# A gated delta attention layer and its feed-forward part on one core: v turned by VectorE, one x buffer, new orders on every engine, phases overlapped

## Chip, core and metric

One core of a Trainium2 chip. The metric is the device time of one execution in microseconds (us). The engines are PE (TensorE), DVE (VectorE), ACT (ScalarE), POOL (GpSimd) and SP (SyncE, which issues all transfers here). Each runs its own list of instructions in order and waits on semaphores that others raise.

## What is computed

The reference, cut to its core (16 sequences of 256 tokens, 256 channels, 32 heads with 64 by 64 state, all float32):

```
qkvz = layernorm(x) @ w_qkvz.T          # per head q, k, v, z
q, k, v = causal depthwise conv of 4 taps along the tokens
g = -exp(A_log) * softplus(a + dt_bias);  beta = sigmoid(b)
q, k = l2norm(q) / 8, l2norm(k)
for each token:                          # state S: 64 x 64 per head
    S = S * exp(g);  delta = (v - k S) * beta
    S = S + k delta;  o = q S
o = o * rsqrt(mean(o*o) + eps) * norm_weight * sigmoid(z)
x = x + layernorm(o @ w_out.T)
x = x + layernorm(down(silu(gate(layernorm(x))) * up(layernorm(x))))
```

## The kernel before, in words

The work is cut in three phases, each a block of code of its own with a barrier behind it. Phase 1 normalizes x, transposes it to `xT_d` in DRAM and computes the gates of all heads. Phase 2 is the attention. It loops over 8 groups of 4 heads and, within a group, over 8 blocks of 512 tokens (2 sequences): 64 steps. Phase 3 is the feed-forward part, 8 blocks of 512 tokens.

A step of phase 2 has 16 units (`G`) of 64 tokens and two heads side by side on the partitions, in chunks c = 0 to 3 of each sequence. Its work, by the names in the code:
- PE `project(s)`, s = 0 to 7: k, q, v and z, two slots each; four matmuls of 512 columns each into a PSUM bank (banks 0 to 3 are shared out by hand). ACT takes the first tap of the convolution out of the bank (`first_tap`); for k and v DVE adds the other three (`conv`, L958), for q ACT writes products (`tap_product`) and POOL adds them (`add_tap`, L703).
- PE `k_tokens`, `v_tokens` (L1174): k and v turned so that tokens lie on the partitions, as 32 small matmuls with a unit matrix for each half. DVE scales them out of PSUM (`scale_k`, `scale_v`).
- PE `scores` (L1193), from which DVE takes `a_mat` and `p_t` (`matrices`). The matrix 1 + A of each unit has to be inverted. Its 16 by 16 blocks go through DRAM to a layout with one block per partition (`units_out`, `units_in`), where DVE does forward substitution, 15 columns of two small operations each (`substitute`, L972 and L976, parts 0 to 5, marked by `sub_done0` to `sub_done5`). ACT turns the result (`turn_units`), it goes back through DRAM (`z_out`, `z_back`), and PE joins the blocks (`join16_inner`, `join16_outer`, `join_inner`, `join_outer`).
- The recurrence over chunks, a chain that runs from engine to engine: PE `solve(c)` (L1250), ACT `delta_out`, PE `advance` (L1260), DVE `new_state` (L1026, L1028) and `decay_state`, PE `key_state` for c + 1 (L1240), DVE `residual` (L1013, L1016), PE `solve(c + 1)`; beside it PE `output` (L1273, L1275).
- PE `sum_squares`, `project_out` (L1288); DVE adds to `acc`, which holds the output of all heads for all tokens in SBUF.
- POOL `differences` (L691), `mask` (L695) and `scale_decays` on the decay matrices, `scale_q`, `clamp`, `end_decays`.

The order of all this is written out by hand. Each engine has a `turn(s)`, where s[0] to s[3] are the four steps in flight, s[0] the newest, and the engine takes from each the pieces in the order in which they stand. `wait_for(engine, semaphore, step, n)` waits for that step's count. So an operation that waits holds back all that stands behind it in the turn of its engine. In the turn before, for one step:

```
wait_for(dve, st_full[1], s[3], 1)
new_state(s[3], 1)
...
substitute(s[2], 5, range(12, 15))
...
residual(s[3], 2)
decay_state(s[3], 2)
...
conv(s[1], 0, banks[2])
```

The x block of a step is loaded to one of two tiles `xT`, and the gates (`gcrow`, `gcb`) to single tiles by `load_gates`.

## Time and profile before

| | |
|---|---|
| median of 3 runs | 3398.41 us (3397.84 to 3399.98) |
| the profiled execution | 3400.17 us, span 3398.1 us |
| mean granted clock of TensorE | 0.985 of full speed |
| PE busy | 3208.9 us, 94% |
| DVE busy | 2460.7 us, 72% |
| ACT busy | 1747.8 us, 51% |
| POOL busy | 1094.2 us, 32% |
| DMA queues | 27.3% of 16 engines' span |

The span is the time from the first to the last instruction that the profiler recorded; the time of an execution is a little longer. Busy shares are means over the three phases. Phase 1 lasts to about 85 us, phase 2 to 3008 us, phase 3 to the end. In a row of the timeline the first number is the start in us from the start of the span, the second the time taken, "xN" the number of instructions merged, and what stands in brackets is how long the engine was idle before it and what released it.

### The profile page before, as it was taken

The numbers are of one execution on the slowest core, as the hardware profiler recorded it, in microseconds if no ns is written. First come the engines' busy times: TensorE is split into PE (matmuls) and PEld (weight loads), VectorE is DVE, ScalarE is ACT, GpSimd is POOL, SyncE is SP. The second block draws the span as 40 slices with busy tenths as digits, with TensorE's granted clock in tenths as the row PEclk, the third lists the DMA queues.
The fourth block names the chain that finished last, engine by engine and source line by source line (L and its number), as shares of the span: only waits on it lengthen the run. The fifth ranks groups of instructions, "written<-read, shape, count | busy, mean of one in ns | idle before, by whom it ended". The sixth has DMA issues, their size and how long they took to land. (4 is left out here: it accounts for less than half of the span.)

```text
span 3398.1 us, 116966 instructions
## 1 busy us (share of the span) xinstructions
PE 3208.9 (94%) x51008; PEld 2185.0 (64%) x51008; DVE 2460.7 (72%) x5802; ACT 1747.8 (51%) x3306; POOL 1094.2 (32%) x904
## 2 busy tenths in 40 slices
PE   6799999999999999999999999999999999879998
PEld 3466666666666666666666666666666666645554
DVE  6577777777777777777777777777777777645555
ACT  5455555555555555555555555555555555423333
POOL 1433333333333333333333333333333333100000
PEclk8899999999999999999999999999999999979999
DMA  5323232232233233322333223222233222110000
GB/s 143 57 50 61 51 52 44 49 66 52 52 52 65 46 51 52 59 49 50 52 68 53 50 46 66 52 44 49 50 68 52 52 52 45 28 56 25 19 19 19
DMA packets 757483, 175.67 MB, mean 52 GB/s; under 512 B 707568, under 2 KB 728432, under 8 KB 755824
## 3 DMA queue, kind: packets, MB, share of 16 engines
q1 hardware_dynamic: 756976, 168.19, 26.4%
q8 instruction: 406, 6.65, 0.8%
q14 instruction: 101, 0.83, 0.1%
HBM read 120.13 MB, written 39.58 MB: 47 GB/s over the span
## 5 line engine op out<-in xcount | busy, mean ns | idle before, releaser
L1164 PE MATMUL bank<-xT,w_sb 128*128 128x512 f32 x2048 | 1020.7, 622 | 13.2 <-DMA xT<-xT_d 8.3
L703 POOL TENSOR_TENSOR kq<-kq,products 128x510 f32<-128x510 f32 (+2 forms) x384 | 445.2, 1166 | 885.7 <-ACT kq L779 600.5
L1164 PEld LDWEIGHTS bank<-xT,w_sb 128*128 128x128 f32 x2048 | 349.7, 190 | 299.7 <-issue 252.9
L958 DVE SCALAR_TENSOR_TENSOR kq<-bank,cw,kq 128x510 f32<-128x510 f32 (+2 forms) x384 | 286.8, 747 | 166.5 <-ACT kq L779 149.1
L691 POOL TENSOR_TENSOR dec_a<-gcrow,gcb 128x1024 f32<-128x1024 f32 x64 | 121.7, 1902 | 835.7 <-DMA gcb<-gcb_d 835.7
L958 DVE SCALAR_TENSOR_TENSOR v_c<-bank,cw,v_c 128x510 f32<-128x510 f32 (+2 forms) x384 | 285.2, 743 | 9.1
L976 DVE TENSOR_TENSOR x_un<-x_un,prod_un 128x15 f32<-128x15 f32 (+7 forms) x960 | 258.3, 269 | 32.9
L972 DVE TENSOR_TENSOR prod_un<-a_un,x_un 128x15 f32<-128x15 f32 (+7 forms) x960 | 255.8, 266 | 31.2 <-DMA a_un<-a_d 4.3
L1193 PE MATMUL bank<-kq 64*64 64x128 f32 x4096 | 271.3, 272 | 5.3 <-issue 2.8
L1288 PE MATMUL bank<-wo,u_sq 128*128 128x256 f32 x1024 | 260.3, 398 | 2.8 <-DVE u_sq L1035 2.8
L785 ACT ACTIVATE products<-bank,cw 128x512 f32<-128x512 f32 x384 | 246.0, 701 | 0.0
L1275 PEld LDWEIGHTS bank<-p_t,delta 64*64 64x64 f32 x4096 | 215.2, 136 | 47.8 <-issue 47.8
L1275 PE MATMUL bank<-p_t,delta 64*64 64x64 f32 x4096 | 243.3, 220 | 0.0
L1273 PEld LDWEIGHTS bank<-q_g,state 64*64 64x64 f32 x3072 | 179.6, 134 | 95.4 <-issue 95.4
L1193 PEld LDWEIGHTS bank<-kq 64*64 64x64 f32 x4096 | 230.7, 134 | 8.5 <-issue 8.5
L838 ACT COPY delta<-bank 128x256 f32<-128x256 f32 x256 | 94.4, 369 | 247.2 <-PE bank L1250 247.2
L1288 PEld LDWEIGHTS bank<-wo,u_sq 128*128 128x128 f32 x1024 | 187.8, 193 | 34.2 <-DVE u_sq L1035 4.4
L1273 PE MATMUL bank<-q_g,state 64*64 64x64 f32 x3072 | 205.8, 226 | 1.1 <-ACT delta L838 1.1
L779 ACT ACTIVATE kq<-bank,cw 128x512 f32<-128x512 f32 x256 | 169.7, 688 | 67.1 <-PE bank L1164 67.1
L1250 PE MATMUL bank<-rhs,z_t 64*64 64x64 f32 x3072 | 128.0, 222 | 72.5 <-DVE rhs L1016 72.5
L1250 PEld LDWEIGHTS bank<-rhs,z_t 64*64 64x64 f32 x3072 | 106.9, 134 | 126.9 <-issue 126.9
L1005 DVE TENSOR_TENSOR a_mat<-bank,dec_a 128x256 f32<-128x256 f32 x256 | 106.4, 416 | 110.1 <-PE bank L1193 110.0
(159 smaller groups left out, 6007.3 us busy)
## 6 DMA issues: line engine op xcount, KB each, us to landing
xT<-xT_d SPq DMA_DIRECT2D x64, 512.0 KB, 3.8
gcrow<-gcrow_d SPq DMA_DIRECT2D x128, 256.0 KB, 4.6
a_d<-a_mat SPq DMA_DIRECT2D x256, 64.0 KB, 2.1
z_t<-z_d SPq DMA_DIRECT2D x256, 64.0 KB, 2.5
w_sb<-in_w_qkvz SPq DMA_DIRECT2D x8, 1024.0 KB, 6.1
x_un<-eye_un SPq DMA_DIRECT2D x64, 128.0 KB, 3.8
a_un<-a_d SPq DMA_DIRECT2D x64, 128.0 KB, 4.7
z_d<-t_un SPq DMA_DIRECT2D x64, 128.0 KB, 3.0
```

What stands on the lines that cost most here:

```text
L703: nc.gpsimd.tensor_tensor(t[:, :, d:SEQ], t[:, :, d:SEQ], prod[:, :, 0:SEQ - d], ALU.add).then_inc(tap_added[i], 1)
L779: ins = nc.scalar.activation(dst, bank[:, :], ACT.Identity, scale=cw_two[m.grp % 2][:, s * TAPS + TAPS - 1:s * TAPS + TAPS])
L785: ins = nc.scalar.activation(products[i % 4][:, :], bank[:, :], ACT.Identity, scale=cw_two[m.grp % 2][:, w:w + 1])
L958: ins = nc.vector.scalar_tensor_tensor(t[:, :, d:SEQ], src[:, :, 0:SEQ - d], cw_two[m.grp % 2][:, w:w + 1], t[:, :, d:SEQ], ALU.mult, ALU.add)
L972: own.need(own.mark(nc.vector.tensor_tensor(prod, a_un[:, j + 1:B, j:j + 1].broadcast_to([P, rows, wid]), x_un[:, j:j + 1, 0:wid].broadcas ...
L976: ins = nc.vector.tensor_tensor(rest, rest, prod, ALU.subtract)
L1164: ins = nc.tensor.matmul(bank[:, :], w_two[m.grp % 2][:, h, s * P:(s + 1) * P], xT[m.par][:, h, :], start=(h == 0), stop=(h == HT - 1))
L1193: ins = nc.tensor.matmul(bank[half, i * P:(i + 1) * P], kq[half, k, s // 2, t0:t0 + C], kq[half, k:q + 1:q - k, s // 2, t0:t0 + C], start= ...
L1250: ins = nc.tensor.matmul(banks[4][half, 256 + i * C:256 + (i + 1) * C], z_t[m.par][half, g, :], rhs[half, i, :] if c else v_r[m.par][half, ...
L1273: nc.tensor.matmul(o, state[c % 2][half, i, :], q_g[m.par][half, g, :], start=True, stop=False)
L1275: ins = nc.tensor.matmul(o, delta[half, i, :], p_t[m.par][half, g, :], start=(c == 0), stop=True)
L1288: ins = nc.tensor.matmul(bank[:, t * HID:(t + 1) * HID], u_sq[:, a, (2 * k + t) * P:(2 * k + t + 1) * P], wo[m.grp % 2][:, a, :], start=(a ...
```

## The change

v is no longer turned by PE. DVE transposes it in blocks of 32 by 32 (`turn_v`) from `v_c` to a new tile `v_x`, and eight transfers per step (`v_turned`) move the blocks from `v_x` to their places in `v_r`, within SBUF; `scale_v` then scales `v_r` in place. There is one tile `xT` instead of two, loaded after projection 5 of the step before. Banks 0 to 3 are given out in turn (`ring`), 18 uses per step instead of 20. The turn of every engine is written in a new order. `solve(0)`, `advance(0)` and `key_state(1)` stand a turn later, with s[3]. The first x block for phase 2 is loaded in phase 1, and the first normalizations and transposes of phase 3, with its weights, are done within the last steps of phase 2 (phase 3 uses other tiles for that).

```
-        xT = [sb(f"xT{i}", [P, HT, TB]) for i in range(2)]
+        xT = sb("xT", [P, HT, TB])
...
-        products = [sb(f"products{i}", [P, TB]) for i in range(4)]
+        product = sb("product", [P, 4, TB])
+        products = [product[:, i, :] for i in range(4)]
...
+        v_x = sb("v_x", [P, G, C])
...
+                    sp.wait_ge(xT_out[0], 8 * NSP)
+                    sp.dma_start(xT[:, :, :].rearrange("p h t -> p (h t)"), xT_d[0]).then_inc(x_T_in, 16)
...
+        def ring(m, place):
+
+            return banks[(18 * m.off + place) % 4]
...
+        wgu = [[flat(xT), flat(product)[:, 0:INTER]], [flat(w_two[1])[:, 0:INTER], flat(w_two[1])[:, INTER:2 * INTER]]]
+        wdn = flat(w_sb).rearrange("p (i h) -> p i h", h=HID)
+        xt = gcrow[:, :, :].rearrange("p g c -> p (g c)").rearrange("p (t h) -> p t h", h=HID)
+        xn = dec_a[:, :, :].rearrange("p g c -> p (g c)").rearrange("p (t h) -> p t h", h=HID)
...
+                        if m.off:
+                            sp.dma_start(xT[:, :, :].rearrange("p h t -> p (h t)"), xT_d[m.index() % NSP]).then_inc(x_T_in, 16)
...
+                        if m.off == STEPS - 1:
+                            sp.dma_start(first_x, x.rearrange("(s t p) h -> s p t h", p=P, t=TT)[0]).then_inc(xr_in, 16)
...
+                    def v_turned(m):
+                        for h in range(2):
+                            for f in range(2):
+                                for t in range(2):
+                                    r, q = D * h + W2 * t, D * h + W2 * f
+                                    sp.dma_start(v_r[m.par][r:r + W2, :, W2 * f:W2 * f + W2], v_x[q:q + W2, :, W2 * t:W2 * t + W2]) \
+                                        .then_inc(v_f_in, 16)
...
-                        if s[3]:
-                            identity_in(s[3])
-                            wait_for(sp, mats_done[0], s[3], 1)
+                        if s[2]:
+                            wait_for(sp, proj_full[5], s[2], 1, back=1)
+                            load_x(s[2])
+                        if s[3]:
+                            wait_for(sp, mats_done[3], s[3], 1)
                             units_out(s[3])
                         if s[2]:
-                            wait_for(sp, qg_done[1], s[2], 1, back=1)
+                            wait_for(sp, eend_done, s[2], 1, back=1)
                             load_gates(s[2])
                         if s[3]:
                             wait_for(sp, a_d_out, s[3], 64)
                             units_in(s[3])
+                            wait_for(sp, vx_done[1], s[3], 1)
+                            v_turned(s[3])
                             wait_for(sp, zt_done, s[3], 1)
                             z_out(s[3])
-                            x_out(s[3])
                             wait_for(sp, z_d_out, s[3], 16)
                             z_back(s[3])
+                            x_out(s[3])
+                        if s[2]:
+                            wait_for(sp, x_d_out, s[2], 16, back=1)
+                            identity_in(s[2])
+                        if s[3]:
                             wait_for(sp, x_d_out, s[3], 16)
                             x_back(s[3])
-                        if s[1]:
-                            load_x(s[1])
 
                     pipeline(sp, turn)
+
+                    for i in proj_full:
+                        sp.wait_ge(proj_full[i], STEPS)
+                    for i in (2, 5):
+                        sp.wait_ge(tap_added[i], STEPS)
+                    for h in range(HT):
+                        for u in range(2):
+                            sp.dma_start(wgu[h][u], w_gu[:, h, u * INTER:(u + 1) * INTER]).then_inc(wf_in, 16)
+                    sp.dma_start(wdn, w_dn).then_inc(wf_in, 16)
 
...
+                    def turn_v(m, a):
+                        ins = nc.vector.transpose(v_x[:, a * GP:(a + 1) * GP, :].rearrange("p g c -> p (g c)"), v_c[:, a, :])
...
 
-                    def scale_v(m, a, bank):
+                    def scale_v(m, a):
                         g = slice(a * GP, (a + 1) * GP)
-                        ins = nc.vector.tensor_tensor(v_r[m.par][:, g, :], bank[:, :].rearrange("p (g c) -> p g c", c=C), col(br[:, g]).broadcast_to([P, GP, C]), ALU.mult)
-                        if a in vr_done:
...
 
+                    def first_transposes():
+                        pe.wait_ge(xn_ready, 1)
+                        for h in range(HT):
+                            for t in range(TT):
+                                ins = nc.tensor.transpose(banks[(5, 4)[h]][:, t * P:(t + 1) * P], first_n[:, t, h * P:(h + 1) * P], ident[:, :])
+                            ins.then_inc(xT_ready, 1)
+
                     def sum_squares(m, a, bank):
+                        if m.off == STEPS - 1 and a == 1:
+                            first_transposes()
                         nc.tensor.matmul(bank[:, :], ones[:, 0, :], u_sq[:, a, :], start=True, stop=True).then_inc(ss_full[a], 1)
 
```

The turns of DVE, POOL and PE, at three places. Names: `x_un` and `prod_un` are the substitution, `rhs` the residual, `s_dec` the decayed state, `kq` the tile of k and q, `st_full`, `ks_full`, `rhs_done` and so on the semaphores.

DVE before, the end of the substitution and what follows:

```order
L972 TENSOR_TENSOR prod_un<-a_un,x_un 128x15
L976 TENSOR_TENSOR x_un<-x_un,prod_un 128x15
L1013 TENSOR_TENSOR rhs<-bank,b_eg 128x256
L1016 TENSOR_TENSOR rhs<-v_r,rhs 128x256
L1019 TENSOR_TENSOR s_dec<-state,e_end 128x256
L958 SCALAR_TENSOR_TENSOR kq<-bank,cw,kq 128x2x255
L958 SCALAR_TENSOR_TENSOR kq<-bank,cw,kq 128x2x254
L958 SCALAR_TENSOR_TENSOR kq<-bank,cw,kq 128x2x253
L1026 TENSOR_TENSOR state<-bank,s_dec 128x256
```

DVE now, from the residual of chunk 1 to new_state 1:

```order
L1121 TENSOR_TENSOR rhs<-v_r,rhs 128x256
L1071 TENSOR_TENSOR prod_un<-a_un,x_un 128x39
L1075 TENSOR_TENSOR x_un<-x_un,prod_un 128x3x13
L1071 TENSOR_TENSOR prod_un<-a_un,x_un 128x28
L1075 TENSOR_TENSOR x_un<-x_un,prod_un 128x2x14
L1071 TENSOR_TENSOR prod_un<-a_un,x_un 128x15
L1075 TENSOR_TENSOR x_un<-x_un,prod_un 128x15
L1056 SCALAR_TENSOR_TENSOR kq<-bank,cw,kq 128x2x255
L1056 SCALAR_TENSOR_TENSOR kq<-bank,cw,kq 128x2x254
L1056 SCALAR_TENSOR_TENSOR kq<-bank,cw,kq 128x2x253
L1129 TENSOR_TENSOR state<-bank,s_dec 128x256
```

Part 5 of the substitution stood ahead of residual 2, whose new_state 1 was done before; now it stands behind residual 1, and conv 1 and new_state 1 stand behind it.

POOL before, from the differences of a step to its mask and the next add:

```order
L691 TENSOR_TENSOR dec_a<-gcrow,gcb 128x1024 [waits gc_in,deca_done]
L703 TENSOR_TENSOR kq<-kq,products 128x2x255 [waits tap_done2]
L703 TENSOR_TENSOR kq<-kq,products 128x2x254 [waits tap_added0]
L703 TENSOR_TENSOR kq<-kq,products 128x2x255 [waits tap_prod3]
L695 TENSOR_TENSOR dec_p<-dec_a,masks 128x1024
L703 TENSOR_TENSOR kq<-kq,products 128x2x254 [waits tap_prod4,tap_added3]
```

POOL now:

```order
L748 TENSOR_TENSOR dec_a<-gcrow,gcb 128x1024 [waits gc_in]
L760 TENSOR_TENSOR kq<-kq,product 128x2x255 [waits tap_done2]
L760 TENSOR_TENSOR kq<-kq,product 128x2x254 [waits tap_prod1,tap_added0]
L760 TENSOR_TENSOR kq<-kq,product 128x2x253 [waits tap_added1]
L752 TENSOR_TENSOR dec_p<-dec_a,masks 128x1024
L760 TENSOR_TENSOR kq<-kq,product 128x2x255 [waits tap_prod3]
```

The three adds of the first half of q now stand together, and the mask behind them, with nothing of the other half between.

PE before, around the turning of v:

```order
L1222 MATMUL bank<-z_t,a_mat 32x32 x31
L1174 MATMUL bank<-masks,v_c 64x64 [waits mats_done1]
L1174 MATMUL bank<-masks,v_c 64x64 x15
L1174 MATMUL bank<-masks,v_c 64x64 [waits mats_done0]
L1174 MATMUL bank<-masks,v_c 64x64 x15
L1231 MATMUL bank<-p,x_top 32x32 [waits p1_done,xtop_done]
```

PE now, from solve 1 to the k tokens; the groups on `v_c` are gone, and key_state 2 waits for `state_done1`, which DVE raises behind conv 1:

```order
L1360 MATMUL bank<-rhs,z_t 64x64 x7
L1278 MATMUL bank<-xT,w_sb 128x512 [waits z_exp0]
L1278 MATMUL bank<-xT,w_sb 128x512
L1370 MATMUL bank<-delta,kt 64x64 [waits delta_done1]
L1370 MATMUL bank<-delta,kt 64x64 x7
L1287 MATMUL bank<-masks,kq 64x64 [waits tap_prod1]
L1287 MATMUL bank<-masks,kq 64x64 x15
L1350 MATMUL bank<-state,kq 64x64 [waits state_done1]
L1350 MATMUL bank<-state,kq 64x64 x7
L1287 MATMUL bank<-masks,kq 64x64 [waits conv_done1]
```

## Rows read from the trace of the kernel before

**Rows 1.** One step: us; busy PE, PEld, DVE, ACT, POOL; clock; DMA share; GB/s.

```profile
1603.25:1647.64 44.39, 43.36 (x774) 30.22 (x773) 34.16 (x81) 24.45 (x46) 16.95 (x14) 1.00 0.29 50
```

**Rows 2.** Timeline of PE in the same step.

```profile
1635.90 2.08 PE L1174 MATMUL bank<-masks,v_c 64*64 64x64 f32 x64
1637.91 1.20 PE L1231 MATMUL bank<-p,x_top 32*32 32x32 f32 x64
1639.04 1.98 PE L1164 MATMUL bank<-xT,w_sb 128*128 128x512 f32 x4
1640.95 0.68 PE L1250 MATMUL bank<-v_r,z_t 64*64 64x64 f32 x16
1641.56 1.99 PE L1288 MATMUL bank<-wo,u_sq 128*128 128x256 f32 x8
```

**Rows 3.** Waits of PE, 184 to 2920 us: us in total, times, longest.

```profile
PE bank L1250 <- DVE rhs L1016: 63.7, 62, 1.0
```

**Rows 4.** Groups of DVE instructions: busy, mean ns, idle before.

```profile
L958 DVE SCALAR_TENSOR_TENSOR kq<-bank,cw,kq 128x510 f32<-128x510 f32 (+2 forms) x384 | 286.8, 747 | 166.5 <-ACT kq L779 149.1
...
L1045 DVE STREAM_TRANSPOSE x_top<-z_t 128x512 f32<-128x512 f32 x64 | 44.6, 697 | 2.1 <-ACT z_t L822 2.1
```

**Rows 5.** DMA issues: count, KB each, median us to landing.

```profile
z_t<-z_d SPq DMA_DIRECT2D x256, 64.0 KB, 2.5
...
gcb<-gcb_d SPq DMA_DIRECT2D x64, 16.0 KB, 5.0
```

**Rows 6.** Timeline of ACT in a steady step.

```profile
1605.36 0.37 ACT L838 COPY delta<-bank 128x256 f32<-128x256 f32 x1 [3.77 <-PE bank L1250]
1605.63 1.06 ACT L763 ACTIVATE dec_a<-dec_p 128x1024 f32<-128x1024 f32 x1
1606.58 0.59 ACT L773 ACTIVATE z_tmp<-bank 128x512 f32<-128x512 f32 x1
...
1607.27 0.63 ACT L804 ACTIVATE l_z<-z_tmp 128x512 f32<-128x512 f32 x1
1607.79 1.84 ACT L785 ACTIVATE products<-bank,cw 128x512 f32<-128x512 f32 x3
1609.50 0.71 ACT L779 ACTIVATE kq<-bank,cw 128x512 f32<-128x512 f32 x1
```

**Rows 7.** Timeline of POOL at three places.

```profile
129.48 1.90 POOL L691 TENSOR_TENSOR dec_a<-gcrow,gcb 128x1024 f32<-128x1024 f32 x1 [11.40 <-DMA gcb<-gcb_d]
...
1610.29 2.50 POOL L703 TENSOR_TENSOR kq<-kq,products 128x510 f32<-128x510 f32 x2 [9.79 <-ACT kq L779]
...
1618.39 2.36 POOL L695 TENSOR_TENSOR dec_p<-dec_a,masks 128x1024 f32<-128x1024 f32 x1
```

**Rows 8.** Timeline of DVE at the same times.

```profile
129.88 1.53 DVE L972 TENSOR_TENSOR prod_un<-a_un,x_un 128x15 f32<-128x15 f32 x1 [4.25 <-DMA a_un<-a_d]
...
1607.88 0.43 DVE L1026 TENSOR_TENSOR state<-bank,s_dec 128x256 f32<-128x256 f32 x1 [1.64 <-PE bank L1260]
...
1610.28 0.22 DVE L972 TENSOR_TENSOR prod_un<-a_un,x_un 128x55 f32<-128x55 f32 x1
1610.54 1.16 DVE L976 TENSOR_TENSOR x_un<-x_un,prod_un 128x55 f32<-128x55 f32 x1
1611.73 1.12 DVE L972 TENSOR_TENSOR prod_un<-a_un,x_un 128x48 f32<-128x48 f32 x1
```

**Rows 9.** Timeline of PE where phase 2 fills.

```profile
169.11 0.68 PE L1240 MATMUL bank<-state,kq 64*64 64x64 f32 x16 [1.69 <-DVE state L1028]
169.72 3.62 PE L1164 MATMUL bank<-xT,w_sb 128*128 128x512 f32 x4
```

**Rows 10.** Timeline of SP and PE at the change to phase 3.

```profile
3008.33 0.39 SPq L1452 DMA_DIRECT2D gcrow<-in_x  x1
...
3020.22 1.97 PE L1634 MATMUL bank<-ident,dec_a 128*128 128x128 f32 x8 [12.87 <-DMA w_sb<-in_w_dn]
3022.86 1.22 PE L1644 MATMUL bank<-q_sq,v_r 128*128 128x512 f32 x1 [0.67 <-ACT q_sq L1494]
```

More of the change, by code:

```diff
@@ L853, in turn @@
                         if s[1]:
-                            wait_for(act, proj_full[1], s[1], 1)
-                            first_tap(s[1], 1, banks[1])
+                            wait_for(act, diff_done, s[1], 1)
+                            magnitudes(s[1])
+                        if s[2]:
+                            wait_for(act, z_clamped[1], s[2], 1)
+                            log_z(s[2], 1)
                         if s[3]:
@@ L948, in _, with moments, normed, first_norms @@
                     own = Own(dve, dve_self)
+                    first = [acc[:, t, :] for t in range(TT)]
+                    def moments():
+                        ks = [own.mark(nc.vector.bn_stats(stats[:, t, :], first[t])) for t in range(TT)]
+                        for t in range(TT):
+                            own.need(ks[t])
+                            k = own.mark(nc.vector.bn_aggr(mv[:, t, :], stats[:, t, :]))
+                        own.need(k)
+                        nc.vector.tensor_scalar(rstd, mv[:, :, 1], EPS_LN, None, ALU.add).then_inc(var_ready, 1)
+                    def normed(dst, n):
+                        dve.wait_ge(rstd_ready, n + 1)
+                        for t in range(TT):
+                            ins = nc.vector.tensor_scalar(dst[:, t, :], first[t], mv[:, t, 0:1], rstd[:, t:t + 1],
+                                                          ALU.subtract, ALU.mult)
+                        return ins
+                    def first_norms():
+                        k = own.mark(normed(at, 0))
+                        dve.wait_ge(xr_in, 16)
+                        own.need(k)
+                        nc.vector.tensor_tensor(acc[:, 0:TT, :], first_x, at, ALU.add).then_inc(x1_done, 1)
+                        dve.wait_ge(x1_done, 1)
+                        dve.sem_inc(dve_gate, 1)
+                        moments()
                     def tail(m):
@@ L1149, in turn @@
                             substitute(s[1], 0, range(0, 2))
+                            wait_for(dve, sub_done[0], s[1], 1)
+                            substitute(s[1], 1, range(2, 4))
+                            wait_for(dve, sub_done[1], s[1], 1)
+                            substitute(s[1], 2, range(4, 6))
+                            wait_for(dve, sub_done[2], s[1], 1)
+                            substitute(s[1], 3, range(6, 9))
+                        if s[2]:
+                            wait_for(dve, st_full[0], s[2], 1)
+                            new_state(s[2], 0)
                         own.turn()
@@ L1294, in turn @@
                         if s[1]:
-                            wait_for(pe, vr_done[0], s[1], 1, back=1)
-                            project(s[1], 6, banks[0])
+                            wait_for(pe, conv_done[0], s[1], 1)
+                            wait_for(pe, tap_done[0], s[1], 1)
+                            project(s[1], 6, ring(s[1], 2))
+                        if s[3]:
+                            wait_for(pe, zoff_done, s[3], 1)
+                            solve(s[3], 0)
+                        if s[1]:
+                            wait_for(pe, conv_done[4], s[1], 1)
+                            wait_for(pe, tap_done[4], s[1], 1)
+                            project(s[1], 2, ring(s[1], 3))
+                        if s[3]:
+                            wait_for(pe, delta_done[0], s[3], 1)
+                            advance(s[3], 0)
+                        if s[1]:
+                            project(s[1], 1, ring(s[1], 0))
                         if s[3]:
                             output(s[3], 0)
+                            wait_for(pe, state_done[0], s[3], 1)
+                            key_state(s[3], 1)
+                        if s[1]:
+                            project(s[1], 3, ring(s[1], 1))
+                        if s[3]:
                             wait_for(pe, rhs_done[1], s[3], 1)
@@ L1456, in store @@
                         sp.dma_start(out.rearrange("(s t p) h -> s p t h", p=P, t=TT)[i], yo).then_inc(y_out, 16)
-                    load(0)
-                    for h in range(HT):
-                        for u in range(2):
-                            sp.dma_start(wgu[h][u], w_gu[:, h, u * INTER:(u + 1) * INTER]).then_inc(wf_in, 16)
-                    sp.dma_start(wdn, w_dn).then_inc(wf_in, 16)
                     load(1)
```

441 lines of the change are left out of this document (205 added, 236 removed).

## The prediction

> **What bounds the kernel now.** I first read busy time over one steady step [rows 1]: PE works 43.36 of 44.39 us, DVE 34.16, ACT 24.45, POOL 16.95. PE bounds, and what it still waits for is one thing: in the list of waits 62 steps each lose 1.03 us before a solve, to DVE's residual (`rhs`, L1016), 63.7 us in all [rows 3]. There are 64 steps; 62 x 44.39 = 2752 us of the span of 3398.1 are such steps. So I price one step, times 62, then the two phase changes. The profiled execution took 3400.17 us, 2.1 above its span and 1.8 above the median of 3398.41; I add 0.3 to a span to get a median.
>
> **The change, part by part, in one step.**
>
> PE loses `v_tokens`: 64 matmuls; from their first start to the next group's is 2.01 us [rows 2]: **-2.01**. Everything else on PE is only reordered. If no wait remained, the old one goes too: **-1.03**, and a step would be 41.35 us.
>
> DVE gets two block transposes of v, 0.70 us each by the same operation on `x_top` [rows 4]; the scaling of v stays, with its input now in SBUF. 34.2 + 1.4 = 35.6 us of work in 41.35: it fits, by the sum. It is hidden if no order puts it in front of PE.
>
> SP gets eight 64 KB transfers per step, in pieces of 128 B, the shape of `z_t<-z_d`, which lands in 2.5 us [rows 5]. Issued at about 0.5 us each behind `units_in`, they land some 7 us after the last of v is turned, and v is not read before the middle of the next step: nothing, with more than 10 us of cover. The single `xT` is loaded after projection 5, 10 us ahead of projection 0: nothing.
>
> **The order around `sub_done5`** is what I think decides. I walk one step of the new order from t = 0, the start of projection 6. On PE a projection takes 1.91 from start to start, and a group of 16 small matmuls 0.61 [rows 2]; output 0 is such a group, and 32 token matmuls are half of v's 64, 1.00. The row before `key_state(2)` is then: projection 6 at 0, solve 0 at 1.91, projection 2 at 2.52, advance 0 at 4.43, projection 1 at 5.04, output 0 at 6.95, key_state 1 at 7.56, projection 3 at 8.17, solve 1 at 10.08, projection 7 at 10.69, advance 1 at 12.60, k tokens 0 at 13.21, **key_state 2 at 14.21**.
>
> ACT: delta 0 goes out when solve 0 has ended, at 2.64; then, with the spacings of [rows 6] (0.27 for delta, 0.95 for 1024 columns, 0.52 for 512, 0.2 for the two small ones, 0.57 for a tap), decays, square_q and log_z end at 5.3, and two products, the exponential, tap 1 and tap 2 follow: tap 2 of q is done at 8.45.
>
> POOL then runs without a gap, since all it needs is there: three adds of q's taps, 1.2 each as a pair takes 2.50, then the mask, 2.36 [rows 7]: **busy from 8.5 to 14.5**.
>
> DVE: accumulate ends at 0.7, nine columns of substitution (18 operations 0.25 apart [rows 8]) last until 5.3, new_state 0 takes 0.43 [rows 8], substitution 4 (6 operations) ends at 7.2, decay 1 at 7.6. The residual waits for key_state 1 (ends 8.24), so its second half is issued at 8.7, and substitution 5 (6 operations) after it. Both of those read two tiles of SBUF. The rows show what such an operation costs while POOL works: 0.22 us becomes 1.16 and 1.12, one behind each of two adds, and 1.53 behind a POOL operation of 1.90 that it ends with, to 0.03 [rows 7, 8]. So DVE gets one operation through per POOL operation. The residual ends at 10.1 behind the first add; substitution 5 gets its first three through behind add 2 (11.1), add 3 (12.3) and the mask (14.6), the last three free, 15.4. Without POOL it would end at 10.6. Behind it stand conv 1 (3 x 0.747 = 2.24 [rows 4]) and new_state 1 (0.43), so PE can start key_state 2 at 18.2 with 0.15 for the handover, not at 14.2: **+4.0**, bounds 3.6 and 4.4 (0.2 on either side for where the first operation slips in, and as much for the walk). The old order had its two collisions here too, and lost 1.9 us on DVE, 1.03 on PE; it had the mask elsewhere.
>
> The Trainium skill (SBUF — State Buffer, Who interferes with whom) says that a VectorE operation with two SBUF inputs and a GpSimd one that reads SBUF exclude each other for a whole instruction; for the mask, which no row here shows against DVE, it is the only direct word. By it the wait is 4.0 us; if two engines merely shared, the step would be 41.35.
>
> ACT's `turn_units` waits for `sub_done5` too, and taps of k behind it come 5 us later; PE, held by the same 4.0, meets them without a new wait. After that, `add_squares` stands next to POOL's scaling of q and the sum of squares waits for it: **+0.3**, between 0 and 0.6 (half an add of POOL).
>
> **The clock.** After 1.69 us of waiting and shortly before that another short one, TensorE's projection group takes 3.62 us where it takes 1.98 [rows 2, 9]; two levels, 1.2 and 2.4 GHz. A step with a wait of 4.0 us would pay something like it each time: 1.64 for a projection; less where small matmuls follow, which also load weights. I take **+1.3**, bounds 0 and 1.7. In the steady stretch now the clock is at full speed [rows 1] with 1.03 us waits. The Trainium skill (TensorE: Matmul & The Clock Gate, The HAM clock gate) ties the fall to a stretch of idleness; read strictly, a wait this long need not contain one, and the sum would be without the 1.3. The row shows a fall after less, so I keep it.
>
> **Phase changes.** Phase 3 starts at 3008.33, its first gate matmul runs at 3022.86 after 12.87 us for `w_dn` and the transposes [rows 10]. Weights and first block are now ready: -14.5. Given back: solve 0, advance 0 and key_state 1 of the last step lose the cover of the output projections (about 2), and the first transposes (1.97 [rows 10], partly under a wait) stand before the last sum of squares: +3.5 in all. The earlier first x load I count at nothing, as gates and decays still come after the barrier. **-11**, bounds -15 and -5.
>
> **Sum.** -2.01 - 1.03 + 4.0 + 0.3 + 1.3 = +2.56 per step; x 62 = +159; -11; +0.3: 3398.1 + 148 = **3546 us**. Its own range by the bounds: 3420 (3.6, 0, 0 and -15) to 3625.
>
> **Rivals.**
> 1. *The stall, but the clock holds.* +1.26 per step: +78 - 11, 3466 us. For it: the wait may be too short or split; against: [rows 9]. 0.16.
> 2. *Other side: DVE gets past POOL.* If ACT is late enough, POOL's burst starts after 10.6, or substitution 5 is through before the mask. The point of decision is tap 2 of q: 8.45 in my walk, 10.6 needed. Then a loss like today's 1.03 remains: -2.01 per step, -125 - 11, 3263 us; with none, 3198. For it: the walk carries errors of some tenths in each of 20 places, POOL's `differences` waits for a gate transfer (5 us from issue, [rows 5]) and holds up ACT when late. Against: `magnitudes` has almost 2 us of slack before it moves tap 2. 0.28.
> 3. *Half of it.* Only the mask or only the adds hit, a wait of 1.9: -1.14 per step, 3316 us. 0.06.
> 4. *The change does not do what it says*: v or `a_un` arrives late behind the eight transfers, and DVE's waits take back just what PE saves, 3.04 per step less the phases' share: 3398 us; for it only the growth in small pieces, against it the cover above. 0.04.
>
> My forecast itself has 0.46. Faster: 2 and 3, 0.34. Within 0.2% (about what a measurement of this kernel can tell from no change): 4, 0.04. Slower: 0.62. The likeliest case gives 3546 with 3420 to 3625 as its own range; for 8 in 10 the range has to take in rival 2's 3263 but not its tail down to 3198 (0.12), and ends at 3600 (0.05 above): 3255 to 3600.
>
> **What would show it.** Right: in the list of waits PE `key_state` waiting for DVE's state some 4 us in each of 62 steps; substitution operations of over 1 us, four to a step where there are two now, one over 2; a step of 46 to 47.5 us; granted clock under 1.00 in steady windows; no PE time on v's transposes; PE's gap at the phase change under 3 us. Wrong if POOL's adds start after substitution 5 has ended, or a small DVE operation inside the mask takes 0.2 us. If the step is near 41.5, the lock was not where I put it; if it is 45.6 with clock 1.00, only the clock term was wrong.

## The result, and the profile after

| | before | after |
|---|---|---|
| median | 3398.12 us (4 runs, 3395.34 to 3399.98) | 3480.27 us (4 runs, 3466.01 to 3485.81) |
| ratio | | 1.0235, 95% interval 1.0212 to 1.0257: slower |
| profiled execution | 3400.17, span 3398.1 us | 3481.44, span 3479.7 us |
| mean granted clock | 0.985 | 0.956 |

The prediction was 3546 (3255 to 3600), slower with 0.62. To see where 81.6 us of span came from, I take the same group of PE in each step, the outer join (`join_outer`), and measure from the start of one to the start of the next. After the change there are 59 steps between the third and the 62nd group, at 244.98 and 2983.18 us: 46.41 us each. Before, between the second and the 63rd at 207.02 and 2932.01 us, 61 steps: 44.67. So a step costs 1.74 us more, 62 x 1.74 = 108, and everything else gives back 26.

The page after, its busy times and its clock in 40 slices:

```profile
PE 3123.6 (90%) x46912; PEld 2137.2 (61%) x46912; DVE 2797.8 (80%) x5930; ACT 1752.6 (50%) x3306; POOL 1128.0 (32%) x904
...
PEclk9999999999999999999999999999999999989999
```

PE has 85 us less work than before and waits more; DVE went from 2460.7 to 2797.8. Two stretches of one step each (columns as in [rows 1]):

```profile
1603.07:1648.82 45.75, 42.05 (x709) 29.46 (x708) 39.41 (x83) 25.12 (x48) 17.47 (x14) 0.96 0.36 60
1648.82:1694.57 45.75, 41.93 (x726) 29.03 (x726) 40.62 (x87) 25.47 (x48) 17.48 (x14) 1.00 0.36 60
```

The clock was 1.00 in [rows 1]; now it is below that in 50 of the 59 steps and whole in nine. PE's longest waits, 400 to 2900 us (total, times, longest), where [rows 3] had 1.0 at a time:

```profile
PE bank L1350 <- DVE state L1129: 191.0, 54, 3.9
...
PE bank L1360 <- DVE rhs L1121: 8.1, 45, 0.2
```

It is `key_state(2)`, once in every step, 191.0 / 54 = 3.54 us. The timelines of PE, POOL and DVE at this place, in the first of the two stretches:

```profile
1611.11 0.68 PE L1370 MATMUL bank<-delta,kt 64*64 64x64 f32 x16
1611.63 1.10 PE L1287 MATMUL bank<-masks,kq 64*64 64x64 f32 x32
1616.43 1.12 PE L1350 MATMUL bank<-state,kq 64*64 64x64 f32 x16 [3.70 <-DVE state L1129]
1617.31 1.94 PE L1287 MATMUL bank<-masks,kq 64*64 64x64 f32 x32
```

```profile
1607.76 3.63 POOL L760 TENSOR_TENSOR kq<-kq,product 128x510 f32<-128x510 f32 x3 [11.22 <-ACT kq L845]
1611.35 2.35 POOL L752 TENSOR_TENSOR dec_p<-dec_a,masks 128x1024 f32<-128x1024 f32 x1
```

```profile
1607.25 0.42 DVE L1121 TENSOR_TENSOR rhs<-v_r,rhs 128x256 f32<-128x256 f32 x1
1607.59 0.19 DVE L1071 TENSOR_TENSOR prod_un<-a_un,x_un 128x39 f32<-128x39 f32 x1
1607.82 1.26 DVE L1075 TENSOR_TENSOR x_un<-x_un,prod_un 128x39 f32<-128x39 f32 x1
1609.11 1.11 DVE L1071 TENSOR_TENSOR prod_un<-a_un,x_un 128x28 f32<-128x28 f32 x1
1610.26 0.19 DVE L1075 TENSOR_TENSOR x_un<-x_un,prod_un 128x28 f32<-128x28 f32 x1
1610.48 0.94 DVE L1071 TENSOR_TENSOR prod_un<-a_un,x_un 128x15 f32<-128x15 f32 x1
1611.45 2.28 DVE L1075 TENSOR_TENSOR x_un<-x_un,prod_un 128x15 f32<-128x15 f32 x1
1613.65 2.30 DVE L1056 SCALAR_TENSOR_TENSOR kq<-bank,cw,kq 128x510 f32<-128x510 f32 x3
1615.87 0.41 DVE L1129 TENSOR_TENSOR state<-bank,s_dec 128x256 f32<-128x256 f32 x1
```

Read it from the bottom: PE waits for state 1 (L1129), which stands behind the second convolution of k (L1056), which stands behind substitution part 5. Four of its six operations take 1.26, 1.11, 0.94 and 2.28 us instead of about 0.2. They end at 1609.08, 1610.22, 1611.42 and 1613.73: after one, two and all three of POOL's adds (3.63 / 3 = 1.21 each, the last ends at 1611.39) and with the mask (1613.70). The convolution reads a bank and SBUF; here it runs almost wholly after POOL's burst, and experiment 1 shows it beside POOL's adds with the same 2.30 us. Behind the wait PE's groups of 16 and 32 small matmuls take 1.12 and 1.94 instead of 0.68 and 1.10: the low level of the clock.

### The profile page after: what moved, and what is told of

The parts are those of the page before. It is cut to its first block and busy times, and to the rows that moved or that the text cites. A ratio compares the mean times of both kernels' runs of the same rounds, so it can differ in the third digit from the quotient of the medians.

```text
span 3479.7 us, 109296 instructions
## 1 busy us (share of the span) xinstructions
PE 3123.6 (90%) x46912; PEld 2137.2 (61%) x46912; DVE 2797.8 (80%) x5930; ACT 1752.6 (50%) x3306; POOL 1128.0 (32%) x904
## 5 line engine op out<-in xcount | busy, mean ns | idle before, releaser
L1278 PE MATMUL bank<-xT,w_sb 128*128 128x512 f32 x2048 | 995.0, 614 | 12.6 <-PEq L507 5.2
L760 POOL TENSOR_TENSOR kq<-kq,product 128x510 f32<-128x510 f32 (+2 forms) x384 | 443.7, 1156 | 747.1 <-ACT kq L845 556.2
L1071 DVE TENSOR_TENSOR prod_un<-a_un,x_un 128x15 f32<-128x15 f32 (+7 forms) x960 | 370.5, 386 | 27.9 <-DMA a_un<-a_d 1.5
L1350 PE MATMUL bank<-state,kq 64*64 64x64 f32 x3072 | 144.2, 238 | 221.2 <-DVE state L1129 217.8
L1056 DVE SCALAR_TENSOR_TENSOR v_c<-bank,cw,v_c 128x510 f32<-128x510 f32 (+2 forms) x384 | 286.3, 746 | 33.5 <-ACT v_c L845 24.5
L1056 DVE SCALAR_TENSOR_TENSOR kq<-bank,cw,kq 128x510 f32<-128x510 f32 (+2 forms) x384 | 286.3, 746 | 26.7 <-ACT kq L845 17.5
L1303 PE MATMUL bank<-kq 64*64 64x128 f32 x4096 | 277.1, 277 | 20.3 <-issue 17.1
L1385 PEld LDWEIGHTS bank<-p_t,delta 64*64 64x64 f32 x4096 | 241.2, 148 | 47.0 <-issue 47.0
L1350 PEld LDWEIGHTS bank<-state,kq 64*64 64x64 f32 x3072 | 124.5, 151 | 228.5 <-issue 228.5
L774 POOL TENSOR_TENSOR dec_a<-dec_a,cols 128x1024 f32<-128x1024 f32 x64 | 121.7, 1902 | 436.5 <-DVE b_eg L1102 436.4
L851 ACT ACTIVATE product<-bank,cw 128x512 f32<-128x512 f32 x384 | 250.7, 691 | 1.5 <-PE bank L1278 1.5
L771 POOL TENSOR_TENSOR q_g<-kq,gcrow 128x512 f32<-128x512 f32 x128 | 177.3, 1385 | 118.6 <-ACT gcrow L836 113.5
L1383 PEld LDWEIGHTS bank<-q_g,state 64*64 64x64 f32 x3072 | 210.7, 150 | 1.4 <-issue 1.3
```

What stands on the lines that cost most here:

```text
L760: nc.gpsimd.tensor_tensor(t[:, :, d:SEQ], t[:, :, d:SEQ], prod[:, :, 0:SEQ - d], ALU.add).then_inc(tap_added[i], 1)
L771: nc.gpsimd.tensor_tensor(q_g[m.par][:, a * GP:(a + 1) * GP, :], half_of(m, 1)[:, a, :].rearrange("p (g c) -> p g c", c=C), gcrow[:, a * G ...
L851: ins = nc.scalar.activation(products[i % 4], bank[:, :], ACT.Identity, scale=cw_two[m.grp % 2][:, w:w + 1])
L1056: ins = nc.vector.scalar_tensor_tensor(t[:, :, d:SEQ], src[:, :, 0:SEQ - d], cw_two[m.grp % 2][:, w:w + 1], t[:, :, d:SEQ], ALU.mult, ALU.add)
L1071: own.need(own.mark(nc.vector.tensor_tensor(prod, a_un[:, j + 1:B, j:j + 1].broadcast_to([P, rows, wid]), x_un[:, j:j + 1, 0:wid].broadcas ...
L1278: ins = nc.tensor.matmul(bank[:, :], w_two[m.grp % 2][:, h, s * P:(s + 1) * P], xT[:, h, :], start=(h == 0), stop=(h == HT - 1))
```

## The experiments

Twelve runs of eleven kernels, each timed beside the kernel before on the same chip, which took 3396.0 us beside experiments 1 to 4, 3399.7 beside 5 to 8 and 3399.6 beside 9 to 12. The changed kernel was not timed again beside them, so totals are compared with its 3480.27 across chips. "Step" is the mean distance between outer joins from the third to the 62nd.

**1. Substitution part 5 earlier.** In DVE's turn:

```
                             substitute(s[2], 4, range(9, 12))
+                            wait_for(dve, sub_done[4], s[2], 1)
+                            substitute(s[2], 5, range(12, 15))
                         if s[3]:
                             decay_state(s[3], 1)
                             residual(s[3], 1)
-                        if s[2]:
-                            wait_for(dve, sub_done[4], s[2], 1)
-                            substitute(s[2], 5, range(12, 15))
```

> Only DVE's order differs from the changed kernel: substitution part 5 stands right behind part 4, ahead of decay 1 and residual 1. Theory A (part 5 is held by POOL's burst and holds conv 1 and new_state 1): in the changed kernel part 4 ends at 1605.6 and the burst begins at 1607.76, so part 5, 1.3 us without POOL, is through before it; new_state 1 is then done by 1612.2 and PE's wait of 3.5 us at key_state 2 goes, and the cold clock behind it. The step falls from 46.4 us (mean of the steady steps) to 42.0 to 42.8; total 3238 us, 3200 to 3290. Theory B (DVE has too much work since it turns v, and the order only decides where PE waits): a wait of nearly the same length appears elsewhere, at residual 1 or later; total above 3420.

Measured: 3237.92 us, ratio to before 0.9542 (0.9526 to 0.9558), step 42.31. All of the work that the change gave DVE is still there (5930 instructions in both), so theory B falls. DVE's timeline at the same place of a step, and POOL's adds beside it:

```profile
1611.81 0.17 DVE L1075 TENSOR_TENSOR x_un<-x_un,prod_un 128x15 f32<-128x15 f32 x1
...
1612.69 1.04 DVE L1121 TENSOR_TENSOR rhs<-v_r,rhs 128x256 f32<-128x256 f32 x1
1613.65 2.30 DVE L1056 SCALAR_TENSOR_TENSOR kq<-bank,cw,kq 128x510 f32<-128x510 f32 x3
1617.13 0.42 DVE L1129 TENSOR_TENSOR state<-bank,s_dec 128x256 f32<-128x256 f32 x1 [1.18 <-PE bank L1369]
```

```profile
1612.09 3.74 POOL L760 TENSOR_TENSOR kq<-kq,product 128x510 f32<-128x510 f32 x3 [8.70 <-ACT kq L845]
```

Part 5 is through before POOL's burst; at this place only residual 1 is caught by the first add (1.04 instead of 0.42); the convolution takes 2.30 us with the adds beside it; and now DVE waits for PE before state 1 and no longer the other way round. One move of six instructions on DVE is worth 242 us.

**2. The mask later.** In POOL's turn:

```
                             add_tap(s[3], 0, 3)
-                            mask(s[3])
                             add_tap(s[3], 1, 1)
                             add_tap(s[3], 1, 2)
+                            mask(s[3])
```

> Only POOL's order differs from the changed kernel: the mask stands behind the second add of the other half of q, some 10 us later. Theory A: the last operation of substitution part 5, 2.28 us behind the mask, takes 0.2 and ends at about 1611.6, so new_state 1 is done at 1614.2 and PE's wait falls from 3.5 to about 1.5 us; with part of the clock loss gone too, 3320 us, 3290 to 3360. Theory B' (only the three adds matter, or DVE and POOL share the memory): the last operation stays over 1 us and the wait over 2.5: above 3420.

Measured: 3439.45 us, 1.013 (1.0108 to 1.0153), step 45.81. Only 41 us: by the time theory A is wrong here, and the total is above the limit set for B'. The mechanism of A is there all the same, since the last operation of part 5 takes 0.17 us. The list of waits tells what happened:

```profile
PE bank L1350 <- DVE state L1129: 184.3, 109, 1.9
```

The wait at `key_state(2)` did fall, but there are two per step now, of 1.69 us on average. In the step below they are 1.43 us at `key_state(2)` and 1.91 at `key_state(3)`. POOL and DVE in that step:

```profile
1633.79 2.53 POOL L752 TENSOR_TENSOR dec_p<-dec_a,masks 128x1024 f32<-128x1024 f32 x1
```

```profile
1634.04 3.44 DVE L1097 TENSOR_TENSOR v_r<-v_r,cols 128x512 f32<-128x512 f32 x2
...
1638.62 0.38 DVE L1129 TENSOR_TENSOR state<-bank,s_dec 128x256 f32<-128x256 f32 x1
```

Moved, the mask lies beside `scale_v`, whose two operations take 3.44 us instead of 1.28, and state 2 stands behind them. The lock (the hold of one engine by the other for a whole instruction) was not removed but sent to the next place. Experiment 5 tests that reading.

**3. PE kept busy in the wait.**

```
                         ins = tokens(half_of(m, 0), a, bank)
+                        if a == 0:
+                            for extra in range(3):
+                                ins = tokens(half_of(m, 0), a, bank)
                         ins.then_inc(ktok_full[a], 1)
```

> The changed kernel with the first half of k's tokens turned four times into the same bank instead of once, 96 small matmuls or about 2.7 us more of PE work, all of it inside PE's wait of 3.5 us at key_state 2. Theory A (part of the loss is TensorE's clock, which falls while PE waits): the clock stays at 1.00 and the work costs nothing, so the time falls by the clock's share: the steady steps' mean of 46.4 us against 45.7 in one whose clock shows 1.00, 0.7 x 62 = 43, so 3437 us, 3415 to 3465. Theory C (the clock costs nothing, since the small matmuls wait for other engines anyway): 3480, same as the changed kernel, or a little more.

Measured: 3404.02 us, 1.0013 (1.0001 to 1.0026), step 45.02. 96 matmuls more per step, and 76 us less than the changed kernel. The wait and the clock over 2500 us (columns as in [rows 1]; then the list of waits):

```profile
400.00:2900.00 2500.00, 2430.17 (x44748) 1726.48 (x44748) 2226.02 (x4551) 1371.16 (x2557) 985.61 (x783) 1.00 0.37 64
```

```profile
PE bank L1353 <- DVE state L1129: 42.4, 56, 1.1
```

The wait is 0.76 on average, the clock 1.00, where the changed kernel had 0.96. So the clock takes 46.41 - 45.02 = 1.4 us of each step. The total lies below the expected 3415 to 3465: theory A was right in kind, but its 0.7 us a step was half of what the clock costs. The changed kernel's own steps say the same: less their waits, the nine with the whole clock take 40.83 us on average and the other 50 take 42.61, which makes 1.5 us a step over all 59. The runs of both kernels spread little beside that (3466 to 3486 and 3392 to 3410).

**4. Both moves (1 and 2).**

> Both moves together: substitution part 5 ahead of decay 1, and the mask later. Theory A: the waits that each of them removes are the same one, so the two gains don't add: 3230 us, within 1% of the kernel with part 5 early alone. If the gains add up (two separate waits), it is over 80 us below that kernel.

Measured: 3177.9 us, 0.9359 (0.9342 to 0.9376), step 41.39. It is 60 us, 1.9%, below part 5 early alone, more than I allowed for one and the same wait, less than for two separate ones. Why: with part 5 early the mask puts off the adds of the other half of q, the second of them holds up `scale_v` (2.17 us for two operations), and PE waits 0.46 us before `key_state(3)` in each step; with the mask later too, this add starts just behind the last operation of `scale_v` (1.29 us for two), the mask behind both, and that wait is gone:

```profile
PE bank L1349 <- DVE state L1129: 24.4, 53, 0.6
```

```profile
PE bank L1349 <- DVE state L1129: 1.2, 2, 0.6
```

(first of experiment 1, then of this one). The same move of the mask that ran into `scale_v` in experiment 2 misses it here, since DVE is there earlier. A stretch of this kernel as long as a usual step, and its PE at the old place of the wait:

```profile
1611.88:1652.70 40.82, 39.68 (x707) 28.01 (x707) 34.10 (x78) 24.21 (x46) 18.08 (x14) 1.00 0.49 100
```

```profile
1622.77 0.68 PE L1369 MATMUL bank<-delta,kt 64*64 64x64 f32 x16
1623.29 1.10 PE L1286 MATMUL bank<-masks,kq 64*64 64x64 f32 x32
1624.22 0.63 PE L1349 MATMUL bank<-state,kq 64*64 64x64 f32 x16
1624.69 1.10 PE L1286 MATMUL bank<-masks,kq 64*64 64x64 f32 x32
```

Nothing waits there; what is left is 0.26 us before solve 1 in most steps. The kernel beats both that this case began with, by 6.4% and 8.7%.

**5. No mask.** `mask(s[3])` is taken out of the changed kernel's POOL turn, so this kernel leaves out the masking of the decay matrices and does not compute the layer.

> The changed kernel without POOL's mask: the masking of the decay matrices is left out, nothing stands in its place. The run with the mask later got only 41 us, with two waits of 1.7 us where there was one of 3.5; in its trace the mask lies beside the scaling of v, and new_state 2 stands behind that. Theory A (the mask's 2.35 us lock DVE out wherever they lie beside an operation with two SBUF inputs that something stands behind): without the mask the first wait is about 1.5 us and the second one is gone; the step falls from 46.4 to 43.0 us, total 3270 us, 3235 to 3330. Rival (the second wait came from something else, such as the adds that moved): it stays without the mask too, and the total is above 3400.

Measured: 3264.77 us, 0.96 (0.9585 to 0.9615), step 42.76; PE waits 1.43 us before `key_state(2)` (83.1 us over 58) and not before `key_state(3)`. No step has a clock below 1.00. The three adds cost 1.4 us of waiting, the mask the rest and the clock with it. The reading of experiment 2 holds.

**6. The adds wait for residual 1** (on top of 4): `wait_for(pool, rhs_done[1], s[3], 1, back=2)` ahead of the first add.

> The kernel with substitution part 5 early and the mask later, and POOL's first add of q's taps waits for residual 1 to end. What PE still waits for in a steady step there is 0.26 us before solve 1, because residual 1 lies behind the first add (1.03 us instead of 0.42). Theory A: that wait goes, POOL has room for starting 1 us later: -0.26 x 62 = -16, so 3162 us, 3150 to 3172. Rival: the adds, 1 us later, lie beside residual 2 and the scaling of v instead, or the scores wait for them: 3178 or more.

Measured: 3190.27 us, 0.9383 (0.9368 to 0.9398); step 41.49 against 41.39. The wait before solve 1 is gone, and the kernel is 12 us slower than kernel 4 (3187 to 3197 against 3172 to 3183 us). POOL in a step:

```profile
1622.92 4.82 POOL L760 TENSOR_TENSOR kq<-kq,product 128x510 f32<-128x510 f32 x4 [9.28 <-DVE rhs L1122]
1629.30 1.08 POOL L760 TENSOR_TENSOR kq<-kq,product 128x508 f32<-128x508 f32 x1 [1.57 <-ACT product L852]
1630.35 2.81 POOL L752 TENSOR_TENSOR dec_p<-dec_a,masks 128x1024 f32<-128x1024 f32 x1
```

The second half's second add (the second row) holds up `scale_v` (2.21 us for two operations from 1628.73, against 1.29 in kernel 4). Which of the two engines is held hangs on a few hundredths of a us: the last operation of `scale_v` started 0.03 us ahead of this add in kernel 4 (1626.31 against 1626.34), and then the add took 1.60; here it starts 0.03 us behind it. Counted from `new_state(1)` the add comes at the same time as in kernel 4, and `scale_v` 0.06 us later, behind a `decay_state(2)` that took 1.08 us instead of 0.71 beside POOL's fourth add. From 400 to 2700 us `scale_v` is held in 38 of some 55 steps, in kernel 4 in none. So the direction of the rival was right. PE hardly waits for it, though: where PE did not wait for DVE, it waited for its own instructions ("issue"): 37.1 us in 38 waits from 250 to 2700 us, 30.7 in 37 without the gate (waits of 0.2 us and more, here and below), and four steps instead of one have a clock below 1.00. A step lost a wait of 0.24 us on average and is 0.09 longer, so 0.33 us came in elsewhere; these two are some 0.2 of it, the rest is not settled.

**7. v's work back on PE** (on top of 4): as in 3, with `range(2)`, 64 small matmuls.

> The kernel with substitution part 5 early and the mask later, and 64 small matmuls more on PE per step (the first half of k's tokens turned three times into the same bank), as many as PE spent on turning v. If PE's 2.0 us per step for v are on the path once the waits are gone: +2.0 x 64 = +125, so 3300 us, 3285 to 3315. If they lie beside waits on others: under 3220.

Measured: 3360.41 us, 0.9886 (0.987 to 0.9902), step 44.19: +182 us, not +125. The usual undisturbed step went from 40.81 to 42.66 us, 1.9 for the 2.0 expected. Of the 0.9 us on top of that, some 0.6 are PE waiting for instructions:

```profile
PE bank L1316 <- issue: 42.8, 22, 4.1
...
PE bank L1305 <- issue: 16.5, 13, 2.4
```

From 250 to 2700 us these are 59.9 us in 40 waits, against 30.7 in 37. The other 0.35 are the clock: ten of 59 steps have one below 1.00, and in each of them PE had waited 1.7 us or more for instructions; in kernel 4 it is one step. So on a free path 64 matmuls, as many as turned v, cost 1.9 us, and another 0.9 for what they do to the waits and to the clock.

**8. The weights of phase 3 late** (on top of 4): `sp.wait_ge(op_full[1], STEPS)` ahead of their loads.

> The kernel with substitution part 5 early and the mask later, but the weights of phase 3 are issued only when PE has ended the last output projection of phase 2, as far as this part of the change can be undone in one line. PE's gap at the phase change, 1.2 us in the changed kernel and 15.5 before, should be 10 to 14 us: total 3189 us, 3186 to 3193. If the weights were not what the gap of before waited for (but the barrier or the first normalizations, which stay early), under 3182.

Measured: 3184.02 us, 0.9367 (0.935 to 0.9384). The total moved by 6 (by 9 against the second timing of kernel 4). That lies between the two bounds I had set (3186 and 3182) and decides nothing, but the gap itself is in the timeline:

```profile
2806.02 2.07 PE L1722 MATMUL bank<-v_c,xT 128*128 128x512 f32 x2 [11.55 <-DMA w_sb<-in_w_dn]
```

It is 1.18 us with the weights early, so the loads are 10.4 us of the gap. From the end of PE's last output projection to the end of the program it is 386.2 us here and 374.3 to 374.4 in both timings of kernel 4: 11.9 us. The total shows only half of it because the stretch from the 63rd outer join to that point came out at 70.7 us here and at 78.8 and 74.0 in the two timings of kernel 4, although PE's order is the same in all three.

**9. The kernel before, with part 5 behind residual 2.**

```
-                            wait_for(dve, sub_done[4], s[2], 1)
-                            substitute(s[2], 5, range(12, 15))
                         if s[3]:
                             residual(s[3], 2)
+                        if s[2]:
+                            wait_for(dve, sub_done[4], s[2], 1)
+                            substitute(s[2], 5, range(12, 15))
```

> The kernel BEFORE the change, with one move on DVE: substitution part 5 stands behind residual 2 instead of ahead of it. Theory A (the old wait of 1.03 us at solve 2 in each step came from the same lock: two substitution operations held up 1.9 us by POOL's adds, with residual 2 behind them): residual 2 comes 1.3 us earlier and the wait is gone, -1.03 x 62 = -64: 3334 us, 3325 to 3350. Rival (the residual waits for key_state, and the wait stays or moves to new_state 2 or the turned units): 3380 or more.

Measured: 3425.56 us, 1.0084 (1.0058 to 1.0111): a miss, on the side of the rival. The wait of 1.03 at solve 2 is gone, but two others stand in its place, 0.83 and 0.61 in a step:

```profile
PE bank L1176 <- DVE kq L958: 45.4, 55, 0.8
...
PE bank L1262 <- ACT delta L838: 33.9, 56, 0.6
```

The two locked operations are still 1.16 and 1.12 us, and part 5 ends 0.7 us later after the start of POOL's adds (4.81 against 4.13). ACT's `turn_units` waits for it, the taps of k stand behind that, and the convolution (L958) in its turn waited 0.96 us for a tap; the delta comes from ACT too. That this chain makes both waits is read from the timelines, not tested. A wait taken from one consumer was given to others.

**10. One more copy of the tokens only** (as 3, `range(1)`).

> The changed kernel with the first half of k's tokens turned twice instead of once: 32 small matmuls more, so that PE's wait of 3.5 us becomes one of some 2.6. With three times as many (wait 0.75) the clock loss was gone, 1.4 us per step. If the clock falls once a wait is long and holds when it is shorter, the step's mean lies near that of the other run: 3404 to 3430 us. If the loss is the same for any wait of over 2 us: 3475 to 3485. A fall in proportion to the wait would give about 3450.

Measured: 3428.18 us, 1.0081 (1.0049 to 1.0113), runs from 3412 to 3434. The wait is 140.0 / 56 = 2.50 us, the clock 0.98; 37 of 59 steps have the whole clock and take 44.5 us on average, the other 22 take 46.5. So with a wait of 2.5 us the clock falls in some steps, with 3.5 in most, and with 0.76 (experiment 3) in one of 59, which has a second wait of 1.4 us. It lies at the edge of the first of my three cases.

**11. x in two transfers** (on top of 4): `xT[:, 0, :]` where x was loaded, `xT[:, 1, :]` behind a wait for `mats_done[0]`.

> The kernel with substitution part 5 early and the mask later, and the x block is loaded in two transfers of 256 KB, the second one some 3 us after the first. What PE still waits for there is some 28 us in all in which its instructions are late, a few us behind the issue of the 512 KB of x. If that transfer holds up PE's instructions: half of it or more goes, 3150 to 3168 us. If it has nothing to do with it: 3178, and the waits stay at 20 to 30 us.

Measured: 3192.89 us, 0.9396 (0.9376 to 0.9416). The waits for instructions are fewer (20.5 us in 24), but the second half of x came late, four times in this stretch:

```profile
PE bank L1286 <- DMA xT<-xT_d: 9.2, 4, 3.2
```

The total lies outside both ranges. Inconclusive: less than half of those waits went, and the cure cost more (15 us against kernel 4).

**12. Kernel 4 again.**

> The kernel with substitution part 5 early and the mask later once more, beside the run with x in halves: 3178 us, within 0.3%.

Measured: 3175.46 us, 0.9353 (0.9327 to 0.938). It is 2.4 us from the first time; its waits for instructions were 25.3 us, so about 5 us of that kind differ from run to run of one kernel, and the difference that experiment 11 made is hardly more.

## Why the prediction was right, and where its sizes were off

**The stall: right in place and kind, 3.54 us for the 4.0 forecast**, just below the bounds of 3.6 to 4.4. The walk had POOL's burst at 8.5 us after projection 6; counted back from advance 0 at 1603.07, that projection started at 1598.64, so the burst began at 9.12. Residual 1 and the first operation of part 5 slipped in ahead of it, and part 5 ended at 15.1 instead of 15.4. That all three adds and the mask hit was as forecast. The rule of the Trainium skill (SBUF — State Buffer, Who interferes with whom) that the two engines exclude each other for a whole instruction agrees with the trace: 2.28 us for an operation of 0.2 beside a mask of 2.35.

**The old wait of 1.03** as the price of the same lock: its timeline shows it, but experiment 9 could not show that it can be had; the move that I tried opened others.

**PE's own work: -2.01 forecast, more in truth.** Without its waits a step before takes 43.49 us on average, and one of the changed kernel with the whole clock 40.83. That is 2.66 less, where the prediction's terms (-2.01, and +0.3 for `add_squares`) give 1.7: the step of the prediction that was mis-sized is "Everything else on PE is only reordered". v's share is 1.9 (experiment 7). The new order lets groups of small matmuls follow one another directly, and then they start 0.47 to 0.52 us apart, where I took 0.61 for each: without v, the solves, advances, key states, outputs and k tokens of a step take 0.84 us less (five undisturbed steps of kernel 4, against 31 of the kernel before).

**The clock: +1.3 forecast, 1.4 to 1.5 measured** (experiment 3), from one row of another stage. The Trainium skill (TensorE: Matmul & The Clock Gate, The HAM clock gate) ties the fall to idleness, and I had left open whether a wait of 4 us would do. Here it does after 3.5 us in 50 of 59 steps, and after 2.5 us in 22 of 59 (experiment 10).

**`add_squares`: +0.3 forecast, 0.26 measured.** DVE's two additions did collide with `scale_q` (2.36 us for both). The list of waits shows nothing, but PE's group for the sum of squares takes longer (the changed kernel in the step of the timelines above, then the kernel before):

```profile
1631.15 2.25 PE L1400 MATMUL bank<-u_sq,ones 128*128 128x512 f32 x4
```

```profile
1632.85 1.98 PE L1281 MATMUL bank<-u_sq,ones 128*128 128x512 f32 x4
```

In 42 of 59 steps its third matmul starts only when the second addition has ended, 0.06 us behind it, and from the start of this group to the next it is 2.17 us instead of 1.91.

**The step, added up.** The mean step before is 44.67, above the undisturbed one of 44.39 that I priced: 43.49 of work, 1.03 before the solve, 0.15 for late instructions. After: 40.83 of work (with `add_squares`), 3.54 before `key_state(2)`, 0.15 before solve 1, 0.38 for late instructions, 1.51 for the clock, together 46.41. Against the forecast of +2.56, the +1.74 measured has 0.95 less work of PE, 0.3 less waiting for DVE, 0.2 more for the clock and 0.2 more for late instructions, which I had not priced.

**The phases: -11 forecast, about -26 measured**, outside my bounds of -15 and -5. The gap was as forecast: 1.18 us after (L1722 at 3106.44) for 15.5 before, -14.3, and phase 3 is 2 us shorter behind it (375.2 to 373.3). The other -10 lie at the ends of phase 2, where I had a "given back" of +3.5 and nothing for the start. The first outer join is at 156.80 instead of 161.88, -5.1; the 62 steps that follow it, against 62 times their mean, are 1.9 us less than before; and from the 63rd outer join to the end of phase 2 it is 72.5 us (3032.77 to 3105.27) instead of 75.3 (2932.01 to 3007.35), although the first transposes do stand there now and take 1.97 us of PE. How much of these 10 us the change made stays open: the last of the stretches differs by 4.8 us between the two timings of kernel 4 (experiment 8), and the first outer join by 1.6.

So the forecast was 66 us too high: 62 x (2.56 - 1.74) = 51 from the steps, 15 from the phases. (The upper end of its own range adds up to 3620, not 3625.) Rival 1 (the clock holds, 3466) lay nearer in time, but by its mechanism it is excluded, as the clock fell in 50 of 59 steps. Rival 2, DVE past POOL, is what experiment 1 made of the kernel, and its price was right: 3238 measured, 3198 to 3263 forecast. It was reached by DVE's order; the time of ACT's tap, which the prediction named as the point of decision, was not moved in any run.

**What stays open:** why PE's instructions come late more often in the changed kernel (20.1 us, and 30.7 in kernel 4, against 8.7 before, 250 to 2700 us), and whether x's transfer has a part in it; and what the eight transfers of v cost, of which no run was made without them. SyncE takes 8.68 us to issue them in a step (from 1639.12), where the prediction had about 0.5 us each. But nothing waits for them in the lists of waits of the changed kernel and of kernel 4 (400 to 2900 us), and whatever they cost is contained in 41.39 us a step.

## What to carry to other kernels

When work is taken off the bounding engine, look at which pieces of the helping engines now lie side by side: an order that was harmless by its sums can put one locked operation in front of the chain, and what stands behind it in the queue pays. A wait is removed by moving its cause to a time when its partner is idle, and one has to look where that is: the same move of the mask gained 41 us with one order of DVE and 60 us with another. Two engines whose operations start within a few hundredths of a us of each other are no safe order: a small delay turns round which of them is held (experiment 6). Price a wait of a few microseconds on PE with the slow matmuls that follow it.

## What the runs showed of the hardware that was not expected

- The clock's fall is not sure at one length of wait, and it comes after shorter waits than the 3.5 us of the changed kernel. Of 59 steps each, the granted clock was below 1.00 in 50 with one wait of 3.5 us (0.96 over 2500 us), in 22 with one of 2.5 (0.98), in 27 with two of some 1.4 and 1.9 (experiment 2, 0.98), in none with one of 1.4 (experiment 5) and in one with a wait of 0.76 (experiment 3, 1.00). Useless matmuls in a wait made a kernel 76 us faster.
- An operation of DVE that starts just ahead of POOL's is served first (0.19 us at 1607.59 and at 1610.26, between POOL's operations); then POOL holds for its whole instruction. The hold goes both ways: POOL's add took 1.60 us instead of 1.08 when DVE's `scale_v` had started 0.03 us ahead of it (kernel 4). In the changed kernel POOL's adds were little longer for it (three in 3.63 us, two in 2.50 [rows 7]).
- 64 matmuls more in a step of kernel 4 doubled PE's waits for its own instructions (30.7 to 59.9 us) and made ten steps lose clock instead of one, so that 1.9 us of matmuls cost 2.8. It is no rule of their number: with 96 more inside the wait of the changed kernel (experiment 3) these waits were 17.1 us, against 20.1 without.
